# A graph layer with residual and layer norm: sorting the edges first and routing their words through the kept masks

## The chip, the cores and the metric

One core of a Trainium2 chip runs the whole program. The metric is the device time of one execution in microseconds (us). Engines of the core: TensorE (PE), VectorE (DVE), ScalarE (ACT), GpSimd (POOL) and SyncE (SP, which only issues transfers here). Each takes its instructions in order; they meet at semaphores.

## What is computed

100,000 nodes with 128 features, 25,000 edges, f32. With `src` as receiver and `dst` as sender of an edge:

```python
feat = concat([h[rcv], h[snd], rel_pos, distance])       # 128 + 128 + 3 + 1
s1 = silu(feat @ W1 + b1); s2 = silu(s1 @ W2 + b2)
score = (s2 @ W3 + b3)[:, 0]
alpha = softmax of score over the edges of one receiver
msg = h[snd] @ Wv * (alpha * node_weight[snd])[:, None]
y = segment_sum(msg, rcv)
out = layernorm(x + (x + y))                             # per row, eps 1e-5
```

Nodes without an edge get `layernorm(2 x)`. This is called the dense pass below; rows with edges are written over it by a scatter.

## The kernel before

The edges are padded to 25,088 = 49 groups (G) of 4 tiles (TPG) of 128. An indirect DMA on GpSimd gathers or scatters one tile: 128 rows of 512 bytes, whose row numbers lie in one column of an index table. So each pass over the edges is 196 indirect DMAs.

The order of GpSimd is written out in `pool_plan` (L92). First 49 sender groups (`hs`): rows of `xw` (x with the node weight behind it) by `snd_t`, in the edges' given order, into `rec`. Beside it TensorE transposes them, multiplies by `w1b` and the 36-row matrix of edge words (`ef`, split into three bf16 parts), and SP writes records (first-layer part and sender row) to `rec_d` in DRAM. Then receiver groups (`hk`, rows of x by `kg_t`, in sorted order) and record groups (`r`, rows of `rec_d` by `id_t`, in sorted order) alternate. At the end come the scatters (`sc`) of finished rows, behind `dense_written`, which SP raises once, when all dense blocks are stored.

VectorE sorts beside the sender pass: `sort` (L693) is a bitonic network over [128, 256] values that pack key and edge number into one word. A stage (L711) is a minimum and a maximum over 128 columns; a turned stage (L716) is four operations over 64 columns. There are 92 of the one and 28 of the other. Rows are exchanged by 32x32 transposes on VectorE (L748, L754) or through TensorE (L554). `SORT_PLAN` spreads the stages over the turns of the first loop (`i` in `range(B0)`, B0 = 52). Then come the tables: `kg`, `sidx`, `seg`, `far`, `cont` and the row ends.

The second loop has 67 steps (`LAST_STEP`). At step s TensorE does, in this order, the scores of group s-3, the second layer of s-2, the first of s-1, Y of s-11, Z of s-10, and the transposes of receiver rows of s+1 (`turn_rows`, L593). ScalarE copies `hkT`, evaluates `x2`, `x1`, copies `zs` and scales the result rows of an older group (L530). VectorE adds the sum to the rows (L976), takes their statistics, makes the weights `m_q` (L967), and for each batch of four groups a segmented softmax. A step is thus a chain between TensorE, ScalarE and VectorE, pipelined over groups.

The dense pass has 49 blocks (NB) of 2048 rows, each 1 MB in and 1 MB out, in a ring of four (`xin`). SP loads block j at step `DSTEP[j]`-2, VectorE takes statistics (L899) and a 13-step chain for the inverse root (L870 to L884), ScalarE normalises 13 of 16 rows (L478) and VectorE the others (L914) a step later, and SP stores another step later. 17 blocks lie in the first loop, one in three turns; the rest in the second at 8/9 block a step. Sums of receivers that span tiles are corrected at the very end (`fix_in` onward, two more scatters). `link` (L666) is an instruction followed by a wait for itself.

Of the kernel before, what the change touches and what calls it, by code (L numbers as in the profile page):

```python
# [5 lines left out]
F32 = mybir.dt.float32  # L6
BF16 = mybir.dt.bfloat16
I32 = mybir.dt.int32
ALU = mybir.AluOpType
ACT = mybir.ActivationFunctionType  # L10

P = 128
N = 100000
# [8 lines left out]
RW = 2 * H + 1  # L22
# [6 lines left out]
HS_RING, EF_RING, R_RING, X_RING = 12, 4, 12, 4  # L29
# [3 lines left out]
ACT_ROWS = 13  # L33
# [5 lines left out]
LAST_STEP = 67  # L39

SORTW = 256
SROWS = EP // SORTW
PADV = 3.0e38
HALFN, POSB, NEGB = 50000, 37200, 62799
IDBITS = 15
SORT_STEPS = "s" * 91 + "f" + "s" * 6 + "f" + "s" * 8 + "f" + "s" * 7 + "f" + "s" * 8 + "ffsfs"
SORT_FIRST, SORT_LONG, SORT_EACH = 8, 3, 3
# [8 lines left out]
assert SROWS * SORTW == EP and T <= SORTW and EP < 1 << IDBITS and SROWS < P  # L56
assert (HALFN - POSB) >> 8 > 0 and NEGB < 255 << 8 and N - POSB < 255 << 8 and (NEGB - HALFN + 1) >> 8 > 0


def sort_plan():  # L60

    plan, flips, at = [], [], 0
    while at < len(SORT_STEPS):
        n = 0
        while at + n < len(SORT_STEPS) and n < (SORT_FIRST if len(plan) < SORT_LONG else SORT_EACH):
            n += 1
            if SORT_STEPS[at + n - 1] == "f":
                flips.append(len(plan))
                break
        plan.append(n)  # L70
        at += n
    return plan, flips


SORT_PLAN, FLIP_TURNS = sort_plan()
TABLE_TURN = len(SORT_PLAN)
HK_FROM = G
LEAD = 10
B0 = G + 3
assert TABLE_TURN + 1 < G and len(FLIP_TURNS) == 7  # L80


def dense_plan():

    first = [1 + 3 * j for j in range(17)]
    return first + [B0 + (k * 9) // 8 for k in range(NB - len(first))]


DSTEP = dense_plan()


def pool_plan():  # L92
    order = []
    for g in range(G):
        order.append(("hs", g))
        if g >= HK_FROM:
            order.append(("hk", g - HK_FROM))
    hk, r, sc = G - HK_FROM, 0, 0
    while hk < LEAD:
        order.append(("hk", hk))  # L100
        hk += 1
    while r < G or sc < G:
        if r < G:
            order.append(("r", r))
            r += 1
        if hk < G:
            order.append(("hk", hk))
            hk += 1
        elif sc < G and r == G:
            order.append(("sc", sc))  # L110
            sc += 1
    return order
# [6 lines left out]
def gnn_kernel(nc, x, xw, snd_nat, rcv_nat, id_nat, signs, iota, ef_flat, w1, b1, w2, b2, w3, b3, wv, eye, out):  # L119
    rec_d = nc.dram_tensor("rec_d", (EP, RW), F32).ap()  # L120
# [3 lines left out]
    seg_d = nc.dram_tensor("seg_d", (1, EP), BF16).ap()  # L124
    fixi_d = nc.dram_tensor("fixi_d", (1, T), F32).ap()
# [4 lines left out]
    with ExitStack() as ctx:  # L130
# [16 lines left out]
        id_t = sb("id_t", [P, T], I32)  # L147
# [4 lines left out]
        fixi = sb("fixi", [P, 2], I32)  # L152

        hk = sb("hk", [P, G, TPG, H])
        region = sb("region", [P, R_RING * TPG * RW])
        xin = sb("xin", [P, X_RING, BR, H])
        hkT = sb("hkT", [P, 2, GE])
        x1 = sb("x1", [P, GE])
# [16 lines left out]
        at = [0]  # L175

        def part(size):
            at[0] += size
            return region[:, at[0] - size:at[0]]

        hsT = part(2 * GE).rearrange("p (r e) -> p r e", r=2)
        ef = part(EF_RING * GE // 2).bitcast(BF16).rearrange("p (r e) -> p r e", r=EF_RING)
        sort_a = part(SORTW)
        sort_b = part(SORTW)
        row = {n: part(SORTW) for n in ("key", "id", "next", "neg", "mul", "start", "sidx", "kg", "pos", "seg", "zero")}
        row_i = part(SORTW).bitcast(I32)
        far16 = part(SORTW // 2).bitcast(BF16)
        cont16 = part(SORTW // 2).bitcast(BF16)
        seg16 = part(SORTW // 2).bitcast(BF16)
        edge = part(32)  # L190
        assert at[0] <= R_RING * TPG * RW, at[0]

        hflat = hk[:].rearrange("p g q h -> p (g q h)")
        rec = hflat[:, G * GE - HS_RING * TPG * RW:].rearrange("p (r q w) -> p r q w", r=HS_RING, q=TPG)
        taken = [0]

        def early(size):
            taken[0] += size
            return hflat[:, taken[0] - size:taken[0]]

        efc = early(4 * T)
        efr = early(4 * T)
        efp = early(6 * T).bitcast(BF16).rearrange("p (n e) -> p n e", n=3)
        wp = early(3 * H // 2).bitcast(BF16).rearrange("p (n h) -> p n h", n=3)
        wc = early(H)
        wr = early(H)
        rcv_t = early(T).bitcast(I32)
        idrel = early(T)
        sgn = early(8)
        lane = early(SORTW)  # L210
        key_f = early(T)
        neg_f = early(T)
        sgn_f = early(T)
        m_i = early(T).bitcast(I32)
        id_i = early(T).bitcast(I32)

        xflat = xin[:].rearrange("p r b h -> p (r b h)")
        used = [0]

        def late(size):  # L220
            used[0] += size
            return xflat[:, used[0] - size:used[0]]
# [892 lines left out]
```

## Time and profile before

| | before |
|---|---|
| median of 3 runs | 998.38 us (997.25 to 999.5) |
| the profiled execution's span | 996.1 us |
| busy: PE, DVE, ACT, POOL | 575.9, 573.2, 522.6, 752.3 us |
| indirect DMAs | 786, of them 784 in four passes of 196 |
| moved by DMA | 206 MB, 207 GB/s on average |
| mean granted TensorE clock | 0.82 |

Busy times are those of instructions; GpSimd's don't hold the time in which it issues. The profiled execution is a single one, and its span runs from the first to the last instruction, so it is a little shorter than the timed median. All times in the rows below count from the span's start.

### The profile page before, as it was taken

What the parts mean: (1) busy time and instruction counts of PE and PEld (TensorE: products, weight loads), DVE (VectorE), ACT (ScalarE), POOL (GpSimd) and SP (SyncE); (2) the same over time, 40 slices, a digit from 0 to 9 for tenths busy, and PEclk for the clock granted to TensorE, in tenths of its full rate; (3) what the DMA queues carried; (4) which work ended last, traced back from release to release, by engine and by line L of the source; (5) the groups of instructions that cost most, each with busy time, mean ns of one, the idle gap of its engine ahead of it and who ended that gap; (6) DMA issues with size and microseconds to landing.
All of it is one profiled execution on the core that took longest, in us unless ns stands there. A gap on an engine that the chain in (4) does not pass through costs nothing.

```text
span 996.1 us, 10941 instructions
## 1 busy us (share of the span) xinstructions
PE 575.9 (58%) x2587; PEld 394.8 (40%) x2587; DVE 573.2 (58%) x2275; ACT 522.6 (52%) x1168; POOL 752.3 (76%) x790
## 2 busy tenths in 40 slices
PE   0989999988704457677667666777996600000000
PEld 0656766665502223455445444545675500000000
DVE  6987887773452737597698987953678841000000
ACT  0356655554523756777698979974786630000000
POOL 6777777777777777777777777777777777777777
PEclk9999999999998776788788988878999855555555
DMA  7799999989965877788778878763452231111111
GB/s 208 227 302 315 321 320 333 336 233 311 330 226 161 288 256 245 273 292 268 273 272 283 292 234 317 246 185 91 129 124 79 71 78 53 53 51 52 53 53 45
DMA packets 85079, 206.12 MB, mean 207 GB/s; under 512 B 19797, under 2 KB 56566, under 8 KB 72472
## 3 DMA queue, kind: packets, MB, share of 16 engines
q1 hardware_dynamic: 56728, 140.95, 41.7%
q0 software_dynamic: 28288, 64.48, 22.8%
q8 instruction: 21, 0.34, 0.1%
q14 instruction: 42, 0.34, 0.1%
HBM read 113.16 MB, written 92.31 MB: 206 GB/s over the span
## 4 chain that ended last, share of the span: by engine, by line
POOL 38%; issue 23%; PE 20%; ACT 13%; DVE 5%; DMA 0%; POOLq 0%; ACTq 0%; DVEq 0%
POOL hk L422 23%; POOL out_rows L426 15%; ACT xin L478 6%; PE bank L622 5%; PE bank L638 4%; PE bank L645 3%; PE bank L624 2%; ACT hk L530 2%; PE bank L616 2%; PE bank L609 2%; ACT hkT L501 1%; ACT x L511 1%; ACT zs L521 1%; PE bank L597 1%; DVE dst L899 1%
## 5 line engine op out<-in xcount | busy, mean ns | idle before, releaser
L478 ACT ACTIVATE xin<-xin,drs 128x128 f32<-128x128 f32 x637 | 258.1, 484 | 51.6 <-DVE drs L884 51.5
L422 POOL DMA_INDIRECT hk<-in_xw,snd_t x196 | 188.0, 959 | 62.0 <-issue 59.4
L426 POOL DMA_INDIRECT out_rows<-hk,sidx_t x196 | 188.8, 963 | 59.7 <-issue 59.4
L422 POOL DMA_INDIRECT region<-rec_d,id_t x196 | 186.8, 953 | 59.7 <-issue 59.1
L422 POOL DMA_INDIRECT hk<-in_x,kg_t x196 | 186.6, 952 | 59.7 <-issue 59.7
L899 DVE BATCH_NORM_STATS2 dst<-xin 128x6 f32<-128x256 f32 x392 | 137.0, 414 | 61.6 <-DMA xin<-in_x 61.0
L577 PE MATMUL bank<-w1b,region 128*128 128x128 f32 x392 | 149.1, 484 | 13.8 <-ACT region L488 7.8
L622 PE MATMUL bank<-hkT,w1a 128*128 128x512 f32 x98 | 73.2, 839 | 138.8 <-issue 98.3
L577 PEld LDWEIGHTS bank<-w1b,region 128*128 128x128 f32 x392 | 99.8, 315 | 33.9 <-ACT region L488 10.1
L622 PEld LDWEIGHTS bank<-hkT,w1a 128*128 128x128 f32 x98 | 20.1, 240 | 175.5 <-issue 163.2
L511 ACT ACTIVATE x<-bank,bcol 128x512 f32<-128x512 f32 x49 | 33.5, 683 | 95.0 <-PE bank L624 95.0
L530 ACT ACTIVATE hk<-hk,ers 128x128 f32<-128x128 f32 x196 | 79.6, 483 | 0.8 <-DVE ers L884 0.8
L488 ACT ACTIVATE region<-bank 128x512 f32<-128x512 f32 x49 | 28.9, 589 | 91.4 <-PE bank L584 91.4
L584 PE MATMUL bank<-ident,hk 128*128 128x128 f32 x196 | 54.3, 433 | 21.6 <-DMA w<-hk 16.8
L638 PE MATMUL bank<-wvh,zs 128*128 128x128 f32 x392 | 63.7, 314 | 4.1 <-ACT zs L521 4.1
L967 DVE TENSOR_SCALAR m_q<-krow,kcol,acol 128x128 f32<-128x128 bf16 x196 | 62.4, 354 | 4.6 <-PE bank L645 4.4
L609 PE MATMUL bank<-x,wz 128*16 128x128 f32 x392 | 55.5, 289 | 15.4 <-ACT x L506 9.6
L616 PE MATMUL bank<-x,w2s 128*128 128x512 f32 x98 | 59.0, 686 | 6.8 <-ACT x L511 4.7
L638 PEld LDWEIGHTS bank<-wvh,zs 128*128 128x128 f32 x392 | 57.8, 226 | 6.3 <-ACT zs L521 5.5
L645 PE MATMUL bank<-m_q,region 128*128 128x128 f32 x392 | 57.6, 296 | 0.0
L578 PE MATMUL bank<-w,region 36*128 36x128 bf16 x196 | 55.6, 284 | 0.0
L645 PEld LDWEIGHTS bank<-m_q,region 128*128 128x128 f32 x392 | 54.5, 215 | 0.0
(176 smaller groups left out, 853.0 us busy)
## 6 DMA issues: line engine op xcount, KB each, us to landing
xin<-in_x SPq DMA_DIRECT2D x49, 1024.0 KB, 8.2
out_rows<-xin SPq DMA_DIRECT2D x49, 1024.0 KB, 5.2
rec_d<-hk SPq DMA_DIRECT2D x49, 514.0 KB, 7.7
krow<-seg_d SPq DMA_DIRECT2D x49, 128.0 KB, 3.5
hk<-in_xw,snd_t POOLq DMA_INDIRECT x196, 5.8
hk<-in_x,kg_t POOLq DMA_INDIRECT x196, 3.9
region<-rec_d,id_t POOLq DMA_INDIRECT x196, 3.6
out_rows<-hk,sidx_t POOLq DMA_INDIRECT x196, 2.2
```

The costliest lines, as they stand in the source:

```text
L422: pool.indirect_dma_start(out=to, out_offset=None, in_=frm, in_offset=bass.IndirectOffsetOnAxis(ap=index, axis=0)).then_inc(done, 16)
L426: pool.indirect_dma_start(out=out, out_offset=bass.IndirectOffsetOnAxis(ap=index, axis=0), in_=frm, in_offset=None).then_inc(done, 16)
L478: ins = nc.scalar.activation(xin[:, j % X_RING, n, :], xin[:, j % X_RING, n, :], ACT.Identity, bias=drs[:, j % 2, 1, n:n + 1], scale=drs[: ...
L530: ins = nc.scalar.activation(hk[:, g, q, :], hk[:, g, q, :], ACT.Identity, scale=ers[:, b % 2, 0, n:n + 1], bias=ers[:, b % 2, 1, n:n + 1])
L577: pe.matmul(to, hsT[:, j % 2, q * P:(q + 1) * P], w1b[:], start=True, stop=False)
L609: ins = pe.matmul(bank[3][0:BT, 0:P], wz[:, BT - 1 - n:2 * BT - 1 - n], x2[:, q * P:(q + 1) * P], start=(n == 0), stop=(last and q == TPG ...
L616: pe.matmul(bank[2][:], w2s[:], x1[:], start=True, stop=True).then_inc(S["mm2_done"], 1)
L622: pe.matmul(bank[1][:], w1a[:], hkT[:, g % 2, :], start=True, stop=False, skip_group_check=True)
L638: ins = pe.matmul(bank[Y_BANKS[g % 2]][:, q * P:(q + 1) * P], zs[:, q * P:(q + 1) * P], wvh[:], start=True, stop=True)
L645: ins = pe.matmul(bank[5][:, q * P:(q + 1) * P], rr[:, g % R_RING, q, H:2 * H], m_q[:, g % 2, q, :], start=True, stop=True)
L899: ins = vec.bn_stats(dst[:, n:n + 2, :].rearrange("p j w -> p (j w)"), xin[:, j % X_RING, n:n + 2, :].rearrange("p j h -> p h j"))
L967: ins = vec.tensor_scalar(m_q[:, g % 2, q, :], krow[:, g % KROW_RING, q * P:(q + 1) * P], kcol[:, t:t + 1], acol[:, b % 2, n:n + 1], ALU.i ...
```

## The change

The sort comes first and alone on VectorE. It now sorts plain f32 keys (no edge number packed in), and each stage also writes one byte mask of 128 columns that says which pairs it swapped: one instruction more in a stage, two more in a turned one. GpSimd waits for `kg_t` (`tab_ready`) before its first gather, then gathers 43 receiver groups (`HK_AHEAD`).

Meanwhile five words of each edge (the sender's number and four edge features), in tiles [128, 5 x 256], are sent through the same network: for each of 120 swaps ScalarE copies the words with the halves exchanged into PSUM (`swap_copy`), and VectorE copies them back where the mask is set (`copy_predicated`), in three sets of 2, 2 and 1 words. Turns are VectorE transposes, flips go through TensorE and ScalarE. Out of this come `snd_t` and the edge words, both in sorted order, and so the 49 sender groups are gathered in sorted order straight into the ring `rr`. There are no records, no `rec_d`, no `id_t` and no third gather pass.

There is one loop, of 77 steps. Its TensorE part gains the transposes of the sender rows (into `bank0`, which `turn_rows` uses too), the product with `w1b` and that with `w36` over 512 columns; it loses the four transposes of records into `bank1`. ScalarE gains a copy `hsT` and normalises 12 rows of a block instead of 13, VectorE four. All 49 dense blocks lie in this loop: 37 in its first 62 steps (three in five steps), then twelve, one a step. The row-end correction moves to steps 60 to 67 (`FIX_STEP` = 62). SP counts each stored block in `dense_written`, and each batch of scatters waits for the count that covers its last key (`limit`, read from `lim_d`), NB when this key is at or above row 97,952.

The core of the diff:

```diff
-    first = [1 + 3 * j for j in range(17)]
-    return first + [B0 + (k * 9) // 8 for k in range(NB - len(first))]
+    first = [1 + (5 * j) // 3 for j in range(37)]
+    return first + [first[-1] + 1 + k for k in range(1, NB - len(first) + 1)]
 
 
 DSTEP = dense_plan()
+LAST_STEP = DSTEP[-1] + 4
+FIX_STEP = G + 13
...
+    plan, j = [], 0
+    for m in range(1, 16):
+        if m > 8:
+            row = m - 8
+            plan.append(("turn" if row <= 5 else "flip", 0))
+            plan += [("swap", 1 << b) for b in range(row - 1, -1, -1)]
+            plan.append(("turn" if row <= 5 else "flip", 0))
+        plan += [("swap", 1 << b) for b in range(min(m, 8) - 1, -1, -1)]
+    return plan
...
+    order = [("hk", g) for g in range(HK_AHEAD)]
     for g in range(G):
         order.append(("hs", g))
-        if g >= HK_FROM:
-            order.append(("hk", g - HK_FROM))
...
-    return order
+        if HK_AHEAD + g < G:
+            order.append(("hk", HK_AHEAD + g))
+    return order + [("sc", g) for g in range(G)]
...
             def load_block(j):
-                wait_ring(sp, stored, j - X_RING, 16)
+                if j >= X_RING:
+                    wait_ring(sp, stored, j - X_RING, 16)
+                    sp.sem_inc(S["dense_written"], 1)
...
+                if 2 <= s + 2 < G:
+                    load_ef(s + 2)
+                for j in blocks(s - 2):
+                    store_block(j)
+                for j in blocks(s + 2):
+                    load_block(j)
+            for j in range(NB - X_RING, NB):
+                wait_ring(sp, stored, j, 16)
+                sp.sem_inc(S["dense_written"], 1)
...
+            pool.wait_ge(S["tab_ready"], 1)
+            limit = []
...
+                if kind == "hk":
...
-                elif kind == "r":
...
+                elif kind == "hs":
...
-                        pool.wait_ge(S["rows_out"], 80)
+                        pool.wait_ge(S["snd_ready"], 1)
+                        pool.wait_ge(S["efp_out"], 144)
...
                     for q in range(TPG):
                         t = g * TPG + q
-                        gather(rr[:, g % R_RING, q, :], rec_d, id_t[:, t:t + 1], r_in[g % R_RING])
+                        gather(rr[:, g % R_RING, q, :], xw, snd_t[:, t:t + 1], r_in[g % R_RING])
...
                     if g == 0:
-                        pool.wait_ge(S["dense_written"], 1)
+                        pool.wait_ge(S["sidx_ready"], 1)
+                    if g % BATCH == 0:
+                        pool.wait_ge(S["dense_written"], limit[batch_of(g)])
+                        pool.sem_inc(S["may_scatter"], 1)
...
+            def swap_copy(frm, k, to, j):
+                v, w = (a.rearrange("p (c two j) -> p c two j", two=2, j=j) for a in (frm, to))
+                return nc.scalar.activation(w, v[:, :, ::-1, :], ACT.Copy)
...
+            for kind, j in ROUTE:
+                if kind == "swap":
+                    for k in range(len(SETS)):
+                        if done[k]:
+                            act.wait_ge(moved[k], done[k])
+                        if n_flip:
+                            act.wait_ge(restored[k], n_flip)
+                        swap_copy(words(state[now], k), k, held[k], j).then_inc(copied[k], 1)
+                        done[k] += 1
+                elif kind == "turn":
+                    now = 1 - now
+                    for k in range(len(SETS)):
+                        done[k] += 1
+                else:
+                    n_flip += 1
+                    for k in range(len(SETS)):
+                        act.wait_ge(flipped[k], n_flip)
+                        nc.scalar.activation(words(state[now], k), turned[k], ACT.Copy).then_inc(restored[k], 1)
...
+                n_flip += 1
+                for k, (first, n) in enumerate(SETS):
+                    pe.wait_ge(moved[k], done[k])
+                    if n_flip > 1:
+                        pe.wait_ge(restored[k], n_flip - 1)
+                    for w in range(n):
+                        for h in range(2):
+                            o = w * SORTW + h * P
+                            ins = pe.transpose(turned[k][:, o:o + P], state[now][:, first + w, h * P:(h + 1) * P], ident[:])
+                    ins.then_inc(flipped[k], 1)
...
+                wait(pe, "hsT_ready", g)
...
+                if s < G:
+                    wait(pe, "hkT_ready", s + 1)
+                    wait_ring(pe, r_in, s, 16 * TPG)
+                    for q in range(TPG):
+                        ins = pe.transpose(bank[0][:, q * P:(q + 1) * P], rr[:, s % R_RING, q, 0:H], ident[:])
+                    ins.then_inc(S["hsT_done"], 1)
...
-                    wait(pe, "hkT_ready", g + 1)
-                    wait_ring(pe, r_in, g, 16 * TPG)
+                    wait(pe, "hsT_ready", g + 1)
+                    wait_ring(pe, ef_in, g, 16)
                     wait(pe, "x1_ready", g)
-                    pe.matmul(bank[1][:], w1a[:], hkT[:, g % 2, :], start=True, stop=False, skip_group_check=True)
-                    for q in range(TPG):
-                        ins = pe.matmul(bank[1][:, q * P:(q + 1) * P], rr[:, g % R_RING, q, 0:H], ident[:], is_transpose=True,
-                                        start=False, stop=(q == TPG - 1), skip_group_check=True)
-                    ins.then_inc(S["mm1_done"], 1)
+                    pe.matmul(bank[1][:], w1a[:], hkT[:, g % 2, :], start=True, stop=False)
+                    pe.matmul(bank[1][:], w1b[:], hsT[:, g % 2, :], start=False, stop=False)
+                    pe.matmul(bank[1][:], w36[:], ef[:, g % EF_RING, :], start=False, stop=True).then_inc(S["mm1_done"], 1)
...
+            def stage(frm, to, j, n):
+                (lo, hi), (tlo, thi) = two(frm, j), two(to, j)
+                vec.tensor_tensor(mask_of(n).rearrange("p (c j) -> p c j", j=j), lo, hi, ALU.is_gt)
+                vec.tensor_tensor(tlo, lo, hi, ALU.min)
+                link(vec.tensor_tensor(thi, lo, hi, ALU.max))
...
+                m = mask_of(n).rearrange("p (c j) -> p c j", j=j)
+                lo, hi, tlo, thi, m = (v.rearrange("p (m d n) j -> p m d n j", d=2, n=k // (2 * j)) for v in (lo, hi, tlo, thi, m))
+                for d in (0, 1):
+                    vec.tensor_tensor(m[:, :, d], lo[:, :, d], hi[:, :, d], ALU.is_lt if d else ALU.is_gt)
+                    vec.tensor_tensor(tlo[:, :, d], lo[:, :, d], hi[:, :, d], ALU.max if d else ALU.min)
+                    ins = vec.tensor_tensor(thi[:, :, d], lo[:, :, d], hi[:, :, d], ALU.min if d else ALU.max)
...
+            for kind, j in ROUTE:
+                for k, (_, w) in enumerate(SETS):
+                    if kind == "swap":
+                        dve.wait_ge(copied[k], copies + 1)
+                        m = mask_of(n).rearrange("p (c j) -> p c j", j=j).unsqueeze(2).to_broadcast((P, P // j, 2, j))
+                        for i in range(w):
+                            to, frm = (v[:, i * SORTW:(i + 1) * SORTW].rearrange("p (c two j) -> p c two j", two=2, j=j)
+                                       for v in (words(state[now], k), held[k]))
+                            ins = vec.copy_predicated(to, m, frm)
+                        ins.then_inc(moved[k], 1)
+                        done[k] += 1
+                    elif kind == "turn":
+                        dve.wait_ge(moved[k], done[k])
+                        vec.transpose(words(state[1 - now], k), words(state[now], k)).then_inc(moved[k], 1)
+                        done[k] += 1
...
+            dve.wait_ge(S["flip_done"], 9)
+            to, frm = columns(bank[7][:, 0:T], snd_t)
+            link(vec.tensor_copy(to, frm))
+            dve.sem_inc(S["snd_ready"], 1)
+            for k in range(2):
+                dve.wait_ge(moved[k], done[k])
+            split(state[now][:, 0:4, :], efr, efp)
+            dve.sem_inc(S["efp_ready"], 1)
```

## Rows read from the trace of the kernel before

**Rows 1.** The page: busy times and shares; engines in the chain that ended last

```profile
PE 575.9 (58%) x2587; PEld 394.8 (40%) x2587; DVE 573.2 (58%) x2275; ACT 522.6 (52%) x1168; POOL 752.3 (76%) x790
...
POOL 38%; issue 23%; PE 20%; ACT 13%; DVE 5%; DMA 0%; POOLq 0%; ACTq 0%; DVEq 0%
```

**Rows 2.** Groups by line, GpSimd: busy us, mean ns, idle before, releaser

```profile
L426 POOL DMA_INDIRECT out_rows<-hk,sidx_t x196 | 188.8, 963 | 59.7 <-issue 59.4 <-ACT hk L530 0.3
...
L422 POOL DMA_INDIRECT region<-rec_d,id_t x196 | 186.8, 953 | 59.7 <-issue 59.1 <-PE bank L645 0.6
```

**Rows 3.** Order of time, VectorE's start: start us, us, what, idle before

```profile
6.73 0.21 DVE L679 CAST hk<-hk 4x128 bf16<-4x128 f32 x1 [5.39 <-DMA hk<-in_w]
```

**Rows 4.** Order of time, VectorE: a turned stage, then full stages

```profile
20.83 0.23 DVE L721 TENSOR_TENSOR region<-region 128x64 f32<-128x64 f32 x1
20.98 0.22 DVE L722 TENSOR_TENSOR region<-region 128x64 f32<-128x64 f32 x1
...
21.50 0.23 DVE L721 TENSOR_TENSOR region<-region 128x64 f32<-128x64 f32 x1
...
160.70 0.29 DVE L713 TENSOR_TENSOR region<-region 128x128 f32<-128x128 f32 x1
160.91 0.28 DVE L714 TENSOR_TENSOR region<-region 128x128 f32<-128x128 f32 x1
161.23 0.30 DVE L713 TENSOR_TENSOR region<-region 128x128 f32<-128x128 f32 x1
```

**Rows 5.** Groups by line, VectorE: a transpose and a copy from PSUM

```profile
L748 DVE STREAM_TRANSPOSE region<-region 128x256 f32<-128x256 f32 x5 | 2.2, 445 | 0.2
...
L765 DVE COPY region<-bank 128x256 f32<-128x256 f32 x4 | 1.7, 419 | 0.3 <-PE bank L554 0.3
```

**Rows 6.** Order of time, VectorE: first and last instruction of the edge tables

```profile
207.12 0.29 DVE L805 COPY region<-region 128x255 f32<-128x255 f32 x1 [2.64 <-PE bank L560]
...
213.07 0.16 DVE L838 TENSOR_SCALAR region<-region 128x2 f32<-128x2 f32 x1
```

**Rows 7.** Groups by line, ScalarE

```profile
L478 ACT ACTIVATE xin<-xin,drs 128x128 f32<-128x128 f32 x637 | 258.1, 484 | 51.6 <-DVE drs L884 51.5
...
L488 ACT ACTIVATE region<-bank 128x512 f32<-128x512 f32 x49 | 28.9, 589 | 91.4 <-PE bank L584 91.4
...
L535 ACT ACTIVATE xin<-xin 128x784 f32<-128x784 f32 x1 | 0.9, 856 | 10.4 <-DVE xin L1035 10.4
```

**Rows 8.** DMA issues: what, queue, count, KB each, median us to landing

```profile
xin<-in_x SPq DMA_DIRECT2D x49, 1024.0 KB, 8.2
out_rows<-xin SPq DMA_DIRECT2D x49, 1024.0 KB, 5.2
...
ef_d<-hk SPq DMA_DIRECT2D x9, 196.0 KB, 3.6
```

**Rows 9.** Order of time, TensorE: one step of the second loop

```profile
711.46 1.02 PE L622 MATMUL bank<-hkT,w1a 128*128 128x512 f32 x2
712.32 0.60 PE L624 MATMUL bank<-ident,region 128*128 128x128 f32 x4
...
717.01 1.02 PE L622 MATMUL bank<-hkT,w1a 128*128 128x512 f32 x2
```

**Rows 10.** Stretches: us, busy of each engine (instructions), granted clock, DMA share, GB/s

```profile
500.00:600.00 100.00, 69.84 (x365) 46.91 (x364) 89.63 (x366) 90.43 (x208) 75.91 (x80) 0.86 0.81 277
700.00:750.00 50.00, 50.00 (x322) 36.73 (x323) 33.48 (x119) 39.54 (x76) 37.86 (x40) 1.00 0.48 123
```

**Rows 11.** Order of time, VectorE: statistics and chain of one dense block

```profile
230.36 2.75 DVE L899 BATCH_NORM_STATS2 dst<-xin 128x6 f32<-128x256 f32 x8 [9.21 <-DMA xin<-in_x]
233.14 0.17 DVE L870 TENSOR_SCALAR cwd<-dst 128x16 f32<-128x16 f32 x1
...
235.87 0.88 DVE L914 TENSOR_SCALAR xin<-xin,drs 128x128 f32<-128x128 f32 x3
```

**Rows 12.** Order of time, ScalarE: the last batch

```profile
778.27 0.60 ACT L521 ACTIVATE zs<-bank 128x512 f32<-128x512 f32 x1 [8.21 <-PE bank L645]
```

## What the change will do to the time

> **What bounds the kernel now.** I read the busy shares of the page first, then the chain of work that ended last, then the groups of instructions by line for GpSimd. GpSimd is busy for three quarters of the span and has the largest part of the chain; TensorE, VectorE and ScalarE all lie between 52% and 58% [rows 1]. The groups show why: GpSimd issues 784 indirect DMAs, 196 of each of four kinds, each of them about 0.96 us long with 0.30 us of issue before it [rows 2]. That is 1.27 us from start to start, and 784 x 1.27 = 996 us is the span. So three quarters of idle time of the other engines cost nothing today: whatever they do is hidden under the four passes of GpSimd (sender gathers, receiver gathers and record gathers interleaved, then scatters).
>
> The profiled span is 996.1 us and the median of the three runs 998.4, so 2.3 us lie around the span. I build the new time as a new span and add 2.
>
> **What is removed.** The record gathers: 196 x 1.27 = 249 us of GpSimd. If GpSimd still set the end, the kernel would be at 996 - 249 = 747 us plus whatever GpSimd has to wait. The rest of this text is about those waits, because the change also puts three things in front of GpSimd that were beside it before: the sort, the routing, and the dense pass that the last scatters now wait for.
>
> **1. The sort, alone in front.** GpSimd's first gather now waits for `tab_ready`. Before, the first VectorE instruction that needs an input starts at 6.73 us [rows 3]; the sort can start about there. A turned stage of four instructions with its wait takes 0.67 us, the next instruction starting 0.13 to 0.15 us after one before; the mask adds two: 0.94 us. A full stage takes 0.53 us with 0.21 us from start to start; one more makes 0.74 us [rows 4]. Of 120 stages 28 are turned and 92 full: 28 x 0.94 + 92 x 0.74 = 26 + 68 = 94 us. Seven sign multiplications (0.40), ten 32x32 transposes (0.48) and four trips through TensorE (a copy of 0.42 [rows 5], two transposes and two waits, 2.3 together as an estimate) add 17 us, the `kg` column 2.5 us. Tables ready at 6.5 + 94 + 17 + 2.5 = **120 us**. A compare that writes bytes isn't in the trace; between nothing (hidden behind its neighbours) and the 0.42 us of a 256-element pass it costs 0 to 50 us over 120 stages; I take the minimum's price, as it reads the same operands.
>
> **2. The routing.** The remaining tables took from 207.1 to 213.1 us with some 3 us ahead of them [rows 6]; I count 10 us, to 130. Then 120 swaps, each of three ScalarE copies (512, 512 and 256 wide) into PSUM and five predicated copies of 256. No predicated copy is in the trace. The nearest row is the copy of 256 from PSUM, 0.42 us; instructions without a wait between them start about 0.08 us before the end of the last [rows 4], so 0.34 us each and 5 x 0.34 = 1.70 us a swap. ScalarE moves 512 in 0.59 us and 784 from SBUF in 0.86 us, hence some 0.63, 0.63 and 0.41 us, overlapped to about 1.4 us a swap [rows 7]: less than VectorE, and with three sets in turn the copy of the next swap (0.63 plus two semaphores) fits beside the other two sets' 1.0 us. So VectorE sets it: 120 x 1.70 = 204 us. Ten turns of three transposes (0.45 us for 256 [rows 5]) add 16, four flips through TensorE and ScalarE 8, the last column 1: 229 us, and `snd_ready` is at **359 us**. Bounds: at the pace of a one-source SBUF pass (0.25) the swaps cost 150 us, with hand-overs that never overlap (1.4 + 1.7) 370 us. I stay near the PSUM row.
>
> The Trainium skill (VectorE: DVE Perf Modes, section The DRAIN you can't avoid) says that the next operation doesn't start until the pipe is empty and that a semaphore costs nothing extra. The stages disagree: inside a stage the second instruction starts 0.21 us after the first, which lasts 0.29 us, and over the wait it is 0.32 us [rows 4]. By the page's rule a predicated copy would cost its full 0.42 us, the swap 2.10 us and the routing 48 us more. The sum goes by the trace.
>
> Meanwhile GpSimd gathers 43 receiver groups, 172 x 1.27 = 218 us, from 120 to 338. So it is covered for 218 of the 239 us, and then waits for the split of the edge words (5 us) and nine writes to `ef_d` (3.6 us to landing each before [rows 8], and now in 512-byte runs, 9 us in all). First sender gather at **373 us**.
>
> **3. The loop of 77 steps.** Steps 0 to 5 each wait for eight gathers, 10.1 us; with the supply behind them step 10 starts 94 us on, at 467. From step 17 to 48 all parts run. TensorE did a step in 5.55 us when nothing held it, at the full granted clock [rows 9, 10]: 711.46 to 717.01. It loses four transposes of 0.60 us and gains four others, and gains the `w1b` product (0.86, as `w1a` from 711.46 to 712.32) and the 36-row bf16 one (0.2, an estimate): 6.6 us. For ScalarE and VectorE I read the stretch from 500 to 600 us: there eight gathers set 10.2 us a step, with 8/9 of a dense block in it, and ScalarE was busy 90.4%, VectorE 89.6%, that is 9.2 and 9.1 us a step [rows 10]. A dense block costs VectorE 2.75 (statistics), 2.73 (chain) and 1.1 (four rows) = 6.5 us [rows 11], and ScalarE 0.405 us a row [rows 7]. At the new 0.6 block a step VectorE falls to 9.1 - 0.29 x 6.5 = 7.2; ScalarE to 9.2 - (11.6 - 7.2) x 0.405 = 7.4, plus the new `hsT` copy 0.6 = 8.0.
>
> No engine's sum is the step, since `bank0` now ties them: ScalarE's copy of `hkT`, then TensorE's sender transposes, products, Y and Z (4.5 us with the hand-over), then ScalarE's `zs`, four result rows (1.6) and again `hkT`. A step without a block is 7.1 us, one with a block 8.9 (twelve rows more on ScalarE), and the softmax of every fourth step adds 2.8 on ScalarE and 4 on VectorE. 0.6 x 8.9 + 0.4 x 7.1 + 0.7 = 8.9; for VectorE's batch steps, which overrun, 9.1. Bounds: 8.2 (ScalarE nearly full) and 10.2 (what the 500 to 600 stretch held with more dense work). Steps 10 to 16 lack the result rows, 7.9 us each. So 467 + 55 + 32 x 9.1 = **813 us**. Steps 49 to 61 lack the first products: 13 x 7.0, and 8 us of idle in the last batch's softmax, as before [rows 12]: **912 us**.
>
> **4. The dense tail.** Twelve blocks are left, one a step. VectorE needs 6.5 us for one, and 2.1 MB of load and store behind landings of 8.2 and 5.2 us [rows 8] at some 300 GB/s 7.0; I take 7.2, 86 us. The row-end correction, moved into steps 64 to 67, lies beside the transfers; if these aren't late, it costs its 12 us of VectorE. The last block's statistics, chain, rows and store add 15. All dense blocks written at **1013 us**.
>
> **5. The scatters behind it.** The sender gathers end about step 43, near 760 us, so 196 scatters alone would end at 760 + 249 = 1009. But a batch waits for a dense count. Batch 10's last key is near 90,100, count 45; batch 11's is near 98,300, above row 97,952 where the last block starts, so the limit is 49: its 16 scatters, batch 12's four and the two corrections, 22 x 1.27 = 28 us, come behind the last block, and 2 us of landing. The span: 1013 + 28 + 2 = 1043; the median **1045 us**.
>
> In short the 249 us saved are spent: 120 us of sort and 35 us of waiting in front of the sender gathers, and at the end GpSimd waits for a loop in which 640 us pass for what was spread over the whole kernel.
>
> **The rivals.** A, faster: the loop packs. VectorE's work behind 373 us is about 515 us, ScalarE's about the same (their busy times now, less sort and record passes, plus `hsT`). At 90% in every stage, as between 500 and 600 us [rows 10], the loop takes 575 us instead of 640, and the kernel is at 975 to 985. For it: the stretch shows that such a load is possible. Against: the first six steps wait for gathers, the tail for transfers, and `bank0` is a new tie. It decides when a middle step is under 8.0 us.
>
> B, far slower: predicated copies or the ping-pong over semaphores. If a swap takes 2.4 us instead of 1.7, the routing is 84 us longer and nothing hides it, since GpSimd runs out of receiver gathers at 338 us: 1130. For it: no such instruction is in the trace; the drain rule above gives 2.10 us, and 1093. Against: rows of the same width and source.
>
> C: the change doesn't do what it says: the count releases nothing early, and all 196 scatters run behind the last block, 1013 + 251 = 1264. Against: counts up to 45 are reached before the tail's last blocks. Small.
>
> **How the numbers follow.** Forecast (1000 to 1090) 0.55, A 0.26, B 0.17, C 0.02. Within A a little ends within 0.2% of 998.4, which is about what a measurement of this kernel can tell from no change. Faster 0.25, same 0.02, slower 0.73. The range takes in the middle of A, about 970, and B up to the drain rule's value and a little more: 970 to 1110.
>
> **What would show it.** The first receiver gather at 115 to 130 us proves step 1; the first sender gather at 360 to 390 step 2, with GpSimd idle some 35 us before it; VectorE's predicated copies at 0.40 to 0.43 us each. Middle steps of 8.8 to 9.5 us prove step 3; `zs` waiting for TensorE in steps without a block shows the tie. GpSimd idle between scatters for `dense_written`, and 22 scatters behind the last store, prove steps 4 and 5. The prediction fails low if steps are near 8 us and the tail's blocks near 6, high if a swap takes over 2 us.

## The result and the profile after

| | before | after |
|---|---|---|
| median of 4 runs | 998.63 us | 1055.86 us |
| after / before | | 1.058 (95% interval 1.056 to 1.059) |
| profiled span | 996.1 us | 1052.1 us |
| moved by DMA | 206 MB | 155 MB |
| instructions of VectorE | 2275 | 3091 |

The kernel became 5.8% slower; 1045 us was predicted. The page, busy times, the granted clock in 40 slices and the engines of the chain that ended last:

```profile
PE 416.9 (40%) x1990; PEld 256.1 (24%) x1990; DVE 818.0 (78%) x3091; ACT 663.9 (63%) x1442; POOL 563.1 (54%) x594
...
PEclk9999999999999998899998999989989855555555
...
DVE 45%; ACT 17%; PE 15%; issue 8%; DMA 7%; POOL 6%; SPq 1%; ACTq 0%; DVEq 0%; POOLq 0%
```

Against [rows 1], GpSimd fell from 752 to 563 us of work and from 38% to 6% of the chain. VectorE has taken its place: 818 us busy and 45% of the chain. GpSimd's three passes, where there were four [rows 2]:

```profile
L421 POOL DMA_INDIRECT region<-in_xw,snd_t x196 | 186.5, 952 | 215.9 <-PE bank L669 130.7
...
L421 POOL DMA_INDIRECT hk<-in_x,kg_t x196 | 185.4, 946 | 174.3 <-DVEq L784 114.9
...
L425 POOL DMA_INDIRECT out_rows<-hk,sidx_t x196 | 189.0, 964 | 96.2 <-issue 58.5
```

Each pass still costs 1.25 us a gather, but now idle time stands ahead of it: 115 us before the first receiver gather, 131 us at the sender gathers (waiting for Z) and 38 us at the scatters (27.7 and 9.9, waiting for dense blocks). GpSimd in order of time, at the first receiver gather, the first sender gather, the first scatter, and the first of the scatters behind the dense tail:

```profile
115.37 1.12 POOL L421 DMA_INDIRECT hk<-in_x,kg_t  x1 [114.92 <-DVEq L784]
...
364.82 0.94 POOL L421 DMA_INDIRECT region<-in_xw,snd_t  x1 [34.55 <-DMA ef_d<-region]
...
762.93 0.98 POOL L425 DMA_INDIRECT out_rows<-hk,sidx_t  x1 [0.30 <-issue]
...
1022.81 0.97 POOL L425 DMA_INDIRECT out_rows<-hk,sidx_t  x1 [9.93 <-SPq L412]
```

These four lines are the prediction's milestones: 120, 373, 760 and 1013 us were forecast, 115, 365, 763 and 1023 came. The stretches show who works in each (sort, routing, middle steps, tail; columns as in [rows 10]):

```profile
0.00:115.00 115.00, 3.74 (x12) 1.64 (x12) 101.91 (x483) 2.71 (x4) 0.20 (x4) 1.00 0.04 10
125.00:356.00 231.00, 11.25 (x46) 8.98 (x46) 219.82 (x639) 184.89 (x370) 155.29 (x165) 1.00 0.22 53
525.00:815.00 290.00, 241.76 (x1197) 145.69 (x1196) 219.99 (x862) 237.56 (x515) 134.82 (x141) 0.92 0.56 183
912.00:1020.00 108.00, 1.61 (x6) 0.86 (x6) 84.96 (x344) 68.27 (x174) 56.41 (x59) 0.50 0.78 283
```

In the first, only VectorE works, 102 of 115 us. In the second VectorE is busy 220 of 231 us and ScalarE 185; TensorE nearly rests. In the middle steps, where [rows 10] had 90% on VectorE and ScalarE, they have 76% and 82%: there the loop isn't full. In the tail TensorE is done; VectorE is busy 85 of 108 us and the DMA engines 78% of the time.

### The profile page after: what moved, and what is told of

It is laid out like the page before. It is cut to its first block, busy times and chain, and to the rows that moved or that the text cites. A ratio compares the mean times of both kernels' runs of the same rounds, so it can differ in the third digit from the quotient of the medians.

```text
span 1052.1 us, 10664 instructions
## 1 busy us (share of the span) xinstructions
PE 416.9 (40%) x1990; PEld 256.1 (24%) x1990; DVE 818.0 (78%) x3091; ACT 663.9 (63%) x1442; POOL 563.1 (54%) x594
## 4 chain that ended last, share of the span: by engine, by line
DVE 45%; ACT 17%; PE 15%; issue 8%; DMA 7%; POOL 6%; SPq 1%; ACTq 0%; DVEq 0%; POOLq 0%
DVE region L860 19%; ACT xin L477 7%; DMA out_rows<-xin 4%; ACT hk L545 3%; DVE dst L924 3%; PE bank L648 3%; PE bank L649 3%; DVE region L711 3%; POOL region L421 2%; PE bank L662 2%; POOL hk L421 2%; DVE region L713 2%; PE bank L641 2%; PE bank L669 2%; DVE region L712 2%
## 5 line engine op out<-in xcount | busy, mean ns | idle before, releaser
L421 POOL DMA_INDIRECT region<-in_xw,snd_t x196 | 186.5, 952 | 215.9 <-PE bank L669 130.7
L477 ACT ACTIVATE xin<-xin,drs 128x128 f32<-128x128 f32 x588 | 237.8, 483 | 73.7 <-DVE drs L909 73.7
L421 POOL DMA_INDIRECT hk<-in_x,kg_t x196 | 185.4, 946 | 174.3 <-DVEq L784 114.9
L484 ACT ACTIVATE bank<-region 128x512 f32<-128x512 f32 x360 | 180.3, 524 | 148.8 <-DVE region L860 116.8
L860 DVE COPY_PREDICATED region<-region,bank 128x256 f32<-128x256 uint8 x600 | 200.8, 472 | 10.0 <-ACT bank L484 9.8
L601 PE MATMUL bank<-ident,region 128*128 128x128 f32 x40 | 9.6, 424 | 204.1 <-DVE region L860 204.1
L641 PE MATMUL bank<-ident,region 128*128 128x128 f32 x196 | 36.8, 318 | 95.7 <-ACT hkT L513 52.4
L648 PE MATMUL bank<-hkT,w1a 128*128 128x512 f32 x98 | 62.6, 727 | 0.0
L649 PE MATMUL bank<-hsT,w1b 128*128 128x512 f32 x98 | 60.2, 702 | 0.0
L601 PEld LDWEIGHTS bank<-ident,region 128*128 128x128 f32 x40 | 8.0, 224 | 205.6 <-DVE region L860 205.6
L521 ACT ACTIVATE hsT<-bank 128x512 f32<-128x512 f32 x49 | 28.9, 590 | 45.6 <-PE bank L641 45.6
L939 DVE TENSOR_SCALAR xin<-xin,drs 128x128 f32<-128x128 f32 x196 | 55.5, 356 | 1.4
L641 PEld LDWEIGHTS bank<-ident,region 128*128 128x128 f32 x196 | 23.8, 156 | 133.8 <-ACT hkT L513 84.9
```

The costliest lines, as they stand in the source:

```text
L421: pool.indirect_dma_start(out=to, out_offset=None, in_=frm, in_offset=bass.IndirectOffsetOnAxis(ap=index, axis=0)).then_inc(done, 16)
L477: ins = nc.scalar.activation(xin[:, j % X_RING, n, :], xin[:, j % X_RING, n, :], ACT.Identity, bias=drs[:, j % 2, 1, n:n + 1], scale=drs[: ...
L484: return nc.scalar.activation(w, v[:, :, ::-1, :], ACT.Copy)
L641: ins = pe.transpose(bank[0][:, q * P:(q + 1) * P], rr[:, s % R_RING, q, 0:H], ident[:])
L648: pe.matmul(bank[1][:], w1a[:], hkT[:, g % 2, :], start=True, stop=False)
L649: pe.matmul(bank[1][:], w1b[:], hsT[:, g % 2, :], start=False, stop=False)
```

## The experiments

Each kernel is the changed one with one edit, unless said otherwise. The time of the changed kernel is 1055.9 us; a ratio is to the kernel before on the same chip.

**Is the sort on the path, and what does a mask cost?** The masks stay zero (one instruction more clears them, 0.3 us of it in front of the sort), so nothing is routed and the scores differ.

```diff
-                vec.tensor_tensor(mask_of(n).rearrange("p (c j) -> p c j", j=j), lo, hi, ALU.is_gt)
```

> The sort's 148 mask instructions are left out (the masks stay zero, so nothing is routed and the scores are wrong); the routing's copies all still run. Theory: a mask instruction costs its issue slot, 56 x 0.135 + 92 x 0.21 = 27 us, and nothing hides the sort: 1029 us. If it were hidden between the minimum and the maximum: 1055 us.

One run: 1024.6 us. GpSimd's wait for VectorE's sort (us in total, times, longest) fell from 114.9 us to this:

```profile
POOL hk L421 <- DVEq L783: 88.9, 1, 88.9
```

26 us earlier at the front, 31 us at the end (29 between the profiled executions): what the sort takes is on the path, and the mask costs its issue slot. The few us more arose in the loop, whose middle steps took 9.41 us here instead of 9.64; what the clock has to do with that is shown below. The changed kernel's turned stage shows the same; compare [rows 4], now with six instructions:

```profile
8.71 0.23 DVE L720 TENSOR_TENSOR region<-region 128x64 uint8<-128x64 f32 x1
8.85 0.22 DVE L721 TENSOR_TENSOR region<-region 128x64 f32<-128x64 f32 x1
...
9.12 0.22 DVE L720 TENSOR_TENSOR region<-region 128x64 uint8<-128x64 f32 x1
```

**What sets the routing?** Two edge features aren't routed here, so the scores differ.

```diff
-SETS = ((0, 2), (2, 2), (4, 1))
+SETS = ((0, 1), (2, 1), (4, 1))
```

> Three of the five words are routed (sets of one word each); two edge features stay unrouted, so scores differ. My theory: VectorE's predicated copies set the routing (five x 0.331 = 1.66 us a swap), so three make about 1.05 us, the routing ends some 70 us earlier, before GpSimd's 43 receiver groups do (330 us), and only GpSimd's wait of 34.6 us can be won, all of it on the path: 1055.9 - 34 = 1022 us. Rival, that the hand-over between ScalarE and VectorE sets a swap: 1.6 us still, and 1050 us. Second rival, that the wait in front is absorbed by the loop behind: 1055 us.

1023.7 us, ratio 1.025 (1.023 to 1.027). The last copy ended at 261.6 us instead of 349.6, and a swap took 0.99 us in the median (1.05 expected). GpSimd no longer waits for `ef_d`, its first sender gather starts at 331.6 us instead of 364.8, and the loop passed nearly the whole of these 33 us on. The predicated copies (count, busy us, mean ns) are here:

```profile
L860 DVE COPY_PREDICATED region<-region,bank 128x256 f32<-128x256 uint8 x360 | 120.4, 425 | 6.8 <-ACT bank L484 6.6
```

In the changed kernel, ScalarE's swap copies by shape and VectorE's predicated ones:

```profile
L484 ACT ACTIVATE bank<-region 128x512 f32<-128x512 f32 x240 | 143.8, 601 | 148.8 <-DVE region L860 116.8 <-DVE region L865 16.8
...
L484 ACT ACTIVATE bank<-region 128x256 f32<-128x256 f32 x120 | 44.4, 370 | 0.0
...
L860 DVE COPY_PREDICATED region<-region,bank 128x256 f32<-128x256 uint8 x600 | 200.8, 472 | 10.0 <-ACT bank L484 9.8
```

and in order of time, VectorE at the routing's start and end:

```profile
125.28 7.07 DVE L860 COPY_PREDICATED region<-region,bank 128x256 f32<-128x256 uint8 x21
...
350.24 0.36 DVE L873 CAST snd_t<-bank 128x196 int32<-128x196 f32 x1 [0.68 <-PE bank L565]
```

21 copies take 7.07 us, 180 in a row 59.7 us: 0.332 us from start to start, though one lasts 0.472 us in the mean. A swap is 1.66 us, 1.70 was predicted, and ScalarE's three copies (0.60, 0.60 and 0.37 us) are hidden: VectorE waited for them 10 us in all.

The prediction gave only half of what the Trainium skill says (VectorE: DVE Perf Modes, The DRAIN you can't avoid): the same section adds that a next operation that isn't held starts earlier. The trace agrees with that half. Had each copy of 0.472 us waited for the end of the one before, 600 of them would have taken 283 us; VectorE was busy 201 us with them.

**What holds the first steps?**

```diff
-HK_AHEAD = 43
+HK_AHEAD = 49
```

> All 49 receiver groups are gathered ahead instead of 43. GpSimd sat idle for 34.6 us before the first sender gather, so six more groups (24 x 1.25 = 30 us) should fit there for nothing, and steps 0 to 5 should no longer wait for eight gathers each. My theory, that the early steps are paced by gathers: step 10 comes 27 us earlier, the time falls from 1055.9 to about 1029 us. Rival, that these steps are held by ScalarE, VectorE and a slow TensorE anyway: at most 5 us, 1051 us.

1031.1 us, ratio 1.032 (1.031 to 1.034). GpSimd's wait before the first sender gather shrank from 34.6 to 4.8 us, step 10 began at 435.3 instead of 457.7 us, and what followed came about as much earlier (step 48 by 21.9 us). The six groups had been put into the one stretch where GpSimd was short of time, behind one where it idled.

**What holds the middle steps?** From step 17 to 48 one took 9.64 us (the `hkT` copies start at 511.0 and 809.9 us, 31 steps). One step in which ScalarE has no rows of a dense block, in order of time:

```profile
599.72 0.58 ACT L513 ACTIVATE hkT<-bank 128x512 f32<-128x512 f32 x1
...
604.77 0.69 ACT L526 ACTIVATE x<-bank,bcol 128x512 f32<-128x512 f32 x1 [3.00 <-PE bank L650]
606.75 0.60 ACT L536 ACTIVATE zs<-bank 128x512 f32<-128x512 f32 x1 [1.29 <-PE bank L669]
607.25 1.64 ACT L545 ACTIVATE hk<-hk,ers 128x128 f32<-128x128 f32 x4
608.79 0.58 ACT L513 ACTIVATE hkT<-bank 128x512 f32<-128x512 f32 x1
```

and TensorE in it:

```profile
600.35 0.79 PE L641 MATMUL bank<-ident,region 128*128 128x128 f32 x4 [1.77 <-ACT hkT L513]
600.93 1.92 PE L648 MATMUL bank<-hkT,w1a 128*128 128x512 f32 x2
602.64 1.78 PE L649 MATMUL bank<-hsT,w1b 128*128 128x512 f32 x2
```

ScalarE waits 3.0 us for the first product and 1.3 us for Z; TensorE had waited 1.8 us for ScalarE's `hkT` before the sender transposes, and its two products ran 1.9 and 1.8 us, at the lower clock, where a step later they took 1.0. The total of that wait between 525 and 815 us:

```profile
PE bank L641 <- ACT hkT L513: 45.3, 28, 3.2
```

The edit gives the sender transposes bank 6; Y keeps bank 4 alone:

```diff
-Y_BANKS = 4, 6
+Y_BANKS = 4, 4
...
-                wait(pe, "hsT_ready", g)
+                wait(pe, "hkT_ready", g)
...
-                    wait(pe, "hkT_ready", s + 1)
+                    wait(pe, "hsT_ready", s)
                     wait_ring(pe, r_in, s, 16 * TPG)
                     for q in range(TPG):
-                        ins = pe.transpose(bank[0][:, q * P:(q + 1) * P], rr[:, s % R_RING, q, 0:H], ident[:])
+                        ins = pe.transpose(bank[6][:, q * P:(q + 1) * P], rr[:, s % R_RING, q, 0:H], ident[:])
...
-                    wait(pe, "y_done", g - 1)
+                    wait(pe, "y_done", g)
```

> The sender transposes get bank 6, Y keeps bank 4 alone, so TensorE no longer waits for the hkT copy of the same step before the sender transposes. My theory, that the tie through bank 0 is what lifts a middle step from about 8.4 us (the busiest engine's sum) to 9.64 us: TensorE's 45 us of waits for hkT between 525 and 815 us go, steps of 9.1 us, 1038 us. Rival, that ScalarE and VectorE in their batch and block steps set it: the step stays at 9.6 us and the time at 1055 us.

1017.8 us, ratio 1.020 (1.018 to 1.022). The step fell to 8.35 us (509.7 to 768.5), more than expected. The 31 middle steps of this kernel, and TensorE's longest wait between 525 and 815 us, which is now for the single Y bank:

```profile
510.00:768.00 258.00, 232.05 (x1233) 150.56 (x1230) 227.51 (x897) 239.10 (x529) 133.01 (x140) 0.95 0.64 209
```

```profile
PE bank L662 <- DVE hk L987: 22.6, 12, 2.8
```

VectorE and ScalarE are back at 88% and 93%, near the 90% of [rows 10], and TensorE's mean clock is higher (0.95 against 0.92). The part of the edit that isn't the tie:

```diff
-Y_BANKS = 4, 6
+Y_BANKS = 4, 4
...
-                    wait(pe, "y_done", g - 1)
+                    wait(pe, "y_done", g)
```

> Y in one bank, the sender transposes still in bank 0: the part of the bank-6 kernel that isn't the tie. Theory, that the tie through bank 0 alone was worth the 38 us: this gives nothing or costs a few us, 1055 to 1062 us. If it gave a good part of the 38 us by itself, the tie isn't the cause.

One run: 1057.9 us, steps of 9.64 us. So the bank that the two transposes share is the cause of the 38 us.

The 31 steps sorted by what ScalarE does in them, and by the granted clock, show where they lie:

| mean us of a step | 19 steps with rows of a block | 12 steps without |
|---|---|---|
| changed kernel | 10.2 | 8.8: six at clock 1.00 took 7.5, six in which it fell took 10.2 |
| bank 6 | 10.3 | 5.2, all at clock 1.00 |

The tie costs nothing in a step with rows of a block, in which ScalarE has the most to do, and 3.6 us in one without. Some 2.3 of them are the chain itself (7.5 against 5.2). The rest comes with TensorE's clock. Here is one step of the changed kernel at the high level and one in which the clock fell to the lower one (1.2 GHz), and TensorE at the second's start:

```profile
675.30:682.60 7.30, 6.72 (x39) 4.41 (x39) 6.61 (x30) 4.39 (x10) 2.53 (x4) 1.00 0.88 320
693.00:704.70 11.70, 11.08 (x39) 7.42 (x40) 11.11 (x52) 5.77 (x12) 1.51 (x2) 0.57 0.59 191
```

```profile
693.62 1.11 PE L641 MATMUL bank<-ident,region 128*128 128x128 f32 x4 [3.21 <-ACT hkT L513]
694.53 1.91 PE L648 MATMUL bank<-hkT,w1a 128*128 128x512 f32 x2
```

The clock fell nine times between 511 and 810 us, each time during such a wait of TensorE for `hkT` (1.8 to 3.2 us) or within 0.5 us of its end; not every such wait was followed by a fall. The six steps took 16 us more than six at the high level. No run holds the waits and the clock apart, so that the waits bring the lower clock about is the likely reading, not a shown one.

**What does the dense pass cost in the loop?** Rows without an edge aren't written here.

```diff
-LAST_STEP = DSTEP[-1] + 4
+LAST_STEP = 70
...
-            return [j for j in range(NB) if DSTEP[j] == u]
+            return []
...
+            sp.sem_inc(S["dense_written"], NB)
...
-            for j in range(NB - X_RING, NB):
-                wait_ring(sp, stored, j, 16)
-                sp.sem_inc(S["dense_written"], 1)
```

> The dense pass is left out (rows without an edge aren't written), the loop has 70 steps. My theory: a middle step falls from 9.64 to 7.1 to 7.4 us (TensorE's chain through bank 0 alone), GpSimd starts the scatters near 690 us and sets the end: about 942 us. If steps stay above 9 us, something else than the dense work beside it holds the loop.

One run: 953.0 us, steps of 7.50 us (942 us and 7.1 to 7.4 were expected), and GpSimd sets the end. TensorE is busy nearly all the time (same columns):

```profile
515.00:730.00 215.00, 206.86 (x1128) 127.59 (x1127) 110.66 (x378) 148.63 (x281) 119.09 (x125) 1.00 0.27 63
```

So with no dense work TensorE's chain holds the step at 7.5 us, as in the changed kernel's steps without a block at the high clock; 0.6 block a step adds 2.1 us with the shared bank, the lower clock included.

**The plan of the blocks.**

```diff
-    first = [1 + (5 * j) // 3 for j in range(37)]
-    return first + [first[-1] + 1 + k for k in range(1, NB - len(first) + 1)]
+    return [1 + (4 * j) // 3 for j in range(NB)]
```

> The 49 dense blocks are spread evenly, three in four steps, so the loop has 69 steps instead of 77 and no tail of one block a step. If a block costs a middle step 4 to 5 us of ScalarE time, the steps up to 61 get 40 us longer in all and the tail 60 us shorter: 1036 us. Rival, that the loop's total is the sum of the work wherever it lies: 1055 us.

1026.4 us, ratio 1.028 (1.026 to 1.030), more than expected: the middle steps took 9.57 us with a quarter more blocks in them, where 10.2 to 10.4 were expected. GpSimd no longer waits for the dense count. Its 198 last transfers run without a gap from 770.8 us on, so the last sender gather sets the time: 8 us later than in the changed kernel, and 38 us of waiting gone. I tried one reason for the short steps, the phase of the step without a block:

```diff
-    return [1 + (4 * j) // 3 for j in range(NB)]
+    return [2 + (4 * j) // 3 for j in range(NB)]
```

> The even dense plan one step later. In the even plan the step in four without a block is the one in which VectorE also has the result rows' chain (s a multiple of 4); shifted by one, that step has a block too, and the free one comes after it. Its middle steps took 9.58 us with 0.75 block a step, against 9.64 with 0.6. If it is this alignment that made the denser plan cost nothing, the shifted plan has steps of 10.1 to 10.4 us and about 1050 us. If the phase is of no account, it takes the even plan's 1026 us plus one step, 1034 us at most.

1033.0 us, ratio 1.031 (1.028 to 1.035), steps of 9.66 us. The phase is of no account; that theory falls. (The 7 us more don't come from the added step: in the profiled execution step 10 was already 8 us late, and one of the four runs took 1027.2 us.) In the even plan most steps repeat as 7.4 without a block, then 8.9, 10.4 to 10.8 and 10.1 to 10.8. Its steps with a block take 10.2 us, as in the changed kernel; of its eight without one, six took 7.4 us at clock 1.00 and two 8.9 at 0.81, against the 7.5 and 10.2 us of the changed kernel's. So a block adds 1.3 us to a step here and not 4 to 5, and in the even plan the lower clock met mostly steps with a block, where it cost less (the mean clock is 0.91 in the middle steps of both). Why it fell there stays open.

**The tail.** The chain of waits between 894 and 1001 us of the changed kernel (start, us, what):

```profile
894.88 11.72 DMA part_d<-part
...
965.82 8.12 DMA out_rows<-xin
974.43 8.39 DMA out_rows<-xin
983.33 8.68 DMA out_rows<-xin
992.51 8.79 DMA out_rows<-xin
```

SP waits for the store it has just issued before it loads the next block into the same place, and the blocks come 8.9 us apart.

```diff
-R_RING, X_RING, EF_RING = 16, 4, 4
+R_RING, X_RING, EF_RING = 16, 5, 4
```

> The ring of dense blocks has five places instead of four, so a load no longer waits for the store issued just before it. If the last blocks (8.9 us apart, stores of 8.1 to 8.8 us one behind the other in the chain) are held by this hand-over, they come 7 us apart and the time falls by 12 us to 1044 us. If the transfers' own rate holds them, nothing changes: 1055 us.

1051.4 us, ratio 1.051 (1.046 to 1.056), against 1.058 (1.056 to 1.059): some 4 us, a third of what was expected and hardly more than the scatter of the runs (1043.8 to 1053.6). The stores' landing between 900 and 1020 us fell from 7.9 to 4.9 us and SP's wait for them before a load is gone, but VectorE and the transfer of `part_d` took over the chain.

**The dense count.**

```diff
-                        pool.wait_ge(S["dense_written"], limit[batch_of(g)])
+                        pool.wait_ge(S["dense_written"], NB)
```

> Every batch of scatters waits for all 49 dense blocks, as the kernel before did, instead of the count that covers its last key. Theory: all 196 scatters and the two corrections then lie behind the last store near 1022 us: 1022 + 198 x 1.26 + 2 = a span of 1274 us and a time near 1277 us. If GpSimd's scatters were held by something else than the count, it would stay near 1056 us.

One run: 1272.0 us. The count is worth 216 us; rival C of the prediction would have been this kernel.

**Put together.** The 49 groups ahead, bank 6 and the even plan:

> 49 receiver groups ahead, bank 6 for the sender transposes, and the even dense plan together. Singly they gave 25, 38 and 29 us. If they are independent: 1055.9 - 92 = 964 us. My theory says that GpSimd becomes the bound, since its 196 scatters all lie behind the last sender gather: that gather comes near 725 us, plus 249 us of scatters: 978 us. Rival, that the middle steps get longer with the denser plan and give half of it back: 1000 us.

975.1 us, ratio 0.977 (0.975 to 0.979): faster than both kernels. GpSimd's scatters now run without a gap behind a pass with idle time in it:

```profile
L424 POOL DMA_INDIRECT out_rows<-hk,sidx_t x196 | 189.2, 965 | 59.8 <-issue 58.5 <-ACT hk L544 1.2
...
L420 POOL DMA_INDIRECT region<-in_xw,snd_t x196 | 185.7, 947 | 171.2 <-PE bank L668 116.0 <-issue 50.0 <-DMA ef_d<-region 5.3
```

So the scatters were moved into that idle time:

```diff
+        if g >= 26:
+            order.append(("sc", g - 26))
-    return order + [("sc", g) for g in range(G)]
+    return order + [("sc", g) for g in range(G - 26, G)]
```

> As the kernel with all three, and the scatters of group g-26 are issued behind the sender gathers of group g, in the time that GpSimd waits for z_ready. If GpSimd's scatter pass is the bound of the kernel with all three, this takes some 115 us of scatters out of the end and leaves the dense end: last block near 920 us, 22 scatters behind it: about 950 us. Rival, that the scatters now hold up the gathers or wait for the dense count in the middle of the loop: no gain, 978 us or more.

949.4 us, ratio 0.951 (0.949 to 0.953), as expected. GpSimd's wait for Z at the sender gathers has shrunk from 116 to 35 us, and at the end it waits for the dense blocks:

```profile
POOL region L422 <- PE bank L670: 34.7, 12, 6.2
POOL out_rows L426 <- SPq L300: 25.2, 2, 19.0
POOL out_rows L426 <- SPq L413: 22.1, 1, 22.1
```

## Why the prediction held, step by step

- **The bound.** Right: with GpSimd's fourth pass gone the gain was spent on waits, at the front, in the loop and in the tail.
- **Step 1, the sort.** 120 us forecast, 115.4 measured; it starts at 6.56 us, and the stages took their slots. The mask at the minimum's price is right (27 us forecast, 26 measured).
- **Step 2, the routing.** The ranges here were widest, 150 to 370 us of swaps; taking the copy from PSUM as nearest and its overlap from the stages gave 204, and 199 came (120 x 1.66). The tables took the forecast 10 us. The first sender gather came at 365 instead of 373 us, and the 35 us of GpSimd's waiting were right. One sign missed: a predicated copy lasts 0.47 us, not 0.40 to 0.43; the sum hung on the distance between starts, 0.33 us, and that was right.
- **Step 3, the loop.** Step 10 came 93 us behind the first sender gather (94 forecast). The middle step was the term that was missized: 9.64 us, not 9.1, and outside the 8.8 to 9.5 that were to prove it. The chain through `bank0` was the right mechanism, but its step without a block was put at 7.1 us, with TensorE's part at the full granted clock; 7.5 came at that clock and 10.2 where it fell, 8.8 in the mean. Over twelve such steps that is 21 us. The 19 steps with a block took 10.2 us; 8.9 and the whole allowance for softmax and batch steps (0.9 us a step) had been put for them, 4 us more than they took. The difference is the 17 us by which 31 steps were missed. The bounds, 8.2 and 10.2, held both 9.64 and the 8.35 of the bank-6 kernel.
- **Step 4, the tail.** 1013 forecast, 1023 measured. From step 48 to the last store 213 us passed, where the sum had 209. The blocks took 8.9 us, not 7.2, at the very end, because of the store that each load waits for, and SP's wait for `part_d` (11.7 us in the chain) wasn't in the sum at all.
- **Step 5, the scatters.** Right: 22 behind the last store, 29 us where 30 were put.
- **Luck.** That 1045 came so near 1056 is in part cancelling. Step 17 began 11 us early, by the sort and the swaps above all; the middle steps lost 17, the tail 4, and the median lies 2 us above the profiled execution.
- **The rivals.** A was to decide below 8.0 us a step; with dense work beside it the step took 9.64 us with the shared bank and 8.35 without. B fell with the swap at 1.66 us. C would have been 1272.

## What to carry to other kernels

When a pass of the bounding engine is removed, add up what was hidden under it: here 249 us of gathers had covered a sort, a loop and a dense pass, and the sort and the loop then stood one behind the other. A buffer shared by two hand-overs of one step can cost more than either engine's sum shows; look for two engines well under full in a stretch where nothing else is late, and sort the steps by kind before explaining their mean: the 38 us lay in 12 steps of 31. And an engine's written-out order should put its work where it idles: six groups of gathers and 23 groups of scatters moved so gave 25 and 26 us.

## What the runs showed of the hardware

- A predicated copy of 256 f32 columns from PSUM under a byte mask starts 0.33 us after its predecessor in both kernels. It lasts 0.47 us in the mean of the changed kernel (0.43 to 0.58) and 0.43 us in the one with single-word sets.
- A compare that writes bytes takes the same 0.29 us for 128 columns as a minimum in f32.
- ScalarE copies 512 columns from SBUF into PSUM in 0.60 us, about the 0.59 us of its copies from PSUM to SBUF [rows 7], and 256 columns in 0.37 us; 0.63 and 0.41 had been estimated.
- TensorE's granted clock fell to the lower level nine times in the 31 middle steps, each time during or just behind a wait of 1.8 to 3.2 us. A pair of matmuls over 512 columns then took 1.9 us instead of 1.0, and a step held by TensorE's chain up to 11.7 us instead of 7.5.
